# A two-block convolution on one core: float32 products in the first 1x1, shorter norm chains, a first 3x3 in pieces

## The reference

```
out = relu(bn(conv1x1(x, w1), g1, be1))        # 512 -> 128 channels
out = relu(bn(conv3x3(out, w2), g2, be2))      # 128 -> 128
out = bn(conv1x1(out, w3), g3, be3)            # 128 -> 512
x   = relu(x + softplus(residual_scale) * out)

out = conv1x1(x, v1) + bias1b
out = conv3x3(out + bias2a, v2) + bias2b
out = conv1x1(out + bias3a, v3) + bias3b
return relu(out * rscale + rbias + x)
```

## Time and profile before

| | us |
|---|---|
| median of 3 runs | 291.74 (290.62 to 291.79) |
| the profiled execution | 290.35, its span 288.3 |
| TensorE busy | 271.6 |
| VectorE busy | 250.2 |
| ScalarE busy | 203.0 |
| GpSimd busy | 15.9 |

### The profile page before, as it was taken

The page is one execution under the profiler, slowest core; times in us unless marked ns, Lnnn a source line. Parts: engine busy times, 40 slices in busy tenths (PEclk is TensorE's granted clock), DMA queues, the critical chain, the costliest instruction groups (busy, mean ns, idle before and its releaser), DMA issues.

```text
span 288.3 us, 4023 instructions
## 1 busy us (share of the span) xinstructions
PE 271.6 (94%) x1534; PEld 253.8 (88%) x1534; DVE 250.2 (87%) x384; ACT 203.0 (70%) x264; POOL 15.9 (6%) x23
## 2 busy tenths in 40 slices
PE   6878999899999998999997999999999999999991
PEld 3668998699999976868796999999999999999991
DVE  3599999999999657789699999999999997979593
ACT  5678883589877549819878783895976949573674
POOL 0000001000000009900000000000000000000000
PEclk9999999999999999999999999999999999999999
DMA  7999901300000010000000000004040050504088
GB/s 229 378 426 422 423 27 50 144 0 2 0 0 2 0 38 2 0 0 3 0 0 0 2 0 2 1 40 183 2 195 28 2 223 0 225 29 195 14 341 316
DMA packets 6818, 28.44 MB, mean 99 GB/s; under 512 B 912, under 2 KB 3472, under 8 KB 5904
## 3 DMA queue, kind: packets, MB, share of 16 engines
q1 hardware_dynamic: 6224, 27.78, 24.2%
q10 hardware_dynamic: 576, 0.41, 0.5%
HBM read 15.35 MB, written 12.85 MB: 98 GB/s over the span
## 4 chain that ended last, share of the span: by engine, by line
PE 79%; DVE 9%; ACT 6%; DMA 3%; issue 1%; SPq 1%; ACTq 0%; DVEq 0%
PE ps L1066 33%; PE ps L1052 18%; PE ps L1018 9%; PE ps L1055 9%; PE ps L1133 4%; DMA x<-x_dram 3%; PE ps L1116 2%; ACT x L556 2%; PE ps L1110 1%; DVE xl L650 1%; DVE xl L875 1%; ACT xh L357 1%; DVE x L870 1%; DVE vf L721 1%; PE ps L1027 1%
## 5 line engine op out<-in xcount | busy, mean ns | idle before, releaser
L511 ACT ACTIVATE x<-x,shift 128x784 f32<-128x784 f32 x32 | 29.9, 946 | 15.4 <-DVE x L870 15.2
L870 DVE SCALAR_TENSOR_TENSOR x<-ps,scale,x 128x784 f32<-128x784 f32 x32 | 32.4, 1030 | 1.3 <-PE ps L1055 1.2
L1066 PE MATMUL ps<-vh,wu0h 128*128 128x364 f32 (+1 forms) x96 | 32.0, 334 | 1.2 <-ACT vh L403 1.2
L1066 PE MATMUL ps<-vh,wu0l 128*128 128x364 f32 (+1 forms) x96 | 32.0, 333 | 0.0
L1066 PE MATMUL ps<-vh,wu1l 128*128 128x364 f32 (+1 forms) x96 | 32.0, 333 | 0.0
L1066 PE MATMUL ps<-vh,wu1h 128*128 128x364 f32 (+1 forms) x96 | 31.9, 333 | 0.0
L912 DVE SCALAR_TENSOR_TENSOR x<-ps,scal,x 128x784 f32<-128x784 f32 x31 | 31.5, 1028 | 0.0
L1066 PE MATMUL ps<-vl,wu0h 128*128 128x364 f32 (+1 forms) x96 | 31.3, 334 | 0.0
L875 DVE TENSOR_TENSOR xl<-x,xh 128x784 fp32r<-128x784 f32 x28 | 26.1, 971 | 5.8 <-ACT xh L518 5.8
L650 DVE TENSOR_TENSOR xl<-x,xh 128x1568 fp32r<-128x1568 f32 x13 | 23.2, 1781 | 1.8 <-ACT xh L357 1.8
L518 ACT ACTIVATE xh<-x 128x1568 fp32r<-128x1568 f32 x14 | 21.1, 1507 | 2.4 <-PE ps L1055 2.4
(11 more groups left out here) (206 smaller groups left out, 714.8 us busy)
## 6 DMA issues: line engine op xcount, KB each, us to landing
x<-x_dram SPq DMA_DIRECT2D x15, 784.0 KB, 8.2
out_dram<-x SPq DMA_DIRECT2D x6, 1568.0 KB, 5.2
out_dram<-x SPq DMA_DIRECT2D x7, 392.0 KB, 2.8
raw<-w_dram SPq DMA_DIRECT2D x1, 1088.0 KB, 5.1
raw<-w_dram SPq DMA_DIRECT2D x1, 576.0 KB, 11.3
raw<-w_dram SPq DMA_DIRECT2D x2, 256.0 KB, 3.1
x<-x_dram ACTq DMA_DIRECT2D x2, 196.0 KB, 4.0
x<-x_dram SPq DMA_DIRECT2D x2, 196.0 KB, 4.2
```

The costliest lines, as they stand in the source:

```text
L511: nc.scalar.activation(x_quad(q, c), x_quad(q, c), ACT.Relu, bias=shift3[:, c:c + 1]).then_inc(x1_ready, 1)
L870: nc.vector.scalar_tensor_tensor(x_quad(q, c), ps[:, bank:bank + 2, 0:N], scale3[:, c:c + 1], x_quad(q, c), ALU.mult, ALU.add).then_inc(s_ ...
L1066: return nc.tensor.matmul(by_row(ps[:, bank, 0:N])[:, :, a:RW - b], wu[part][:, TILE[k] + dw, :], by_row(v[:, k, :])[:, :, b:RW - a], star ...
```

## The change

- First 1x1. Units 0 and 1 are taken as float32 products of all four tiles, with no split; each unit from 2 to 15 takes its tile 0 as a float32 product and splits only tiles 1 to 3. Units 2, 3, 4 and 15 (`TILED`) are split tile by tile, the others three tiles at a time. The float32 tile waits only for the unit's landing, the split tiles for their low halves.
- The taps' transfer moves from behind unit 3 to behind unit 9; their sums move from unit 3 to units 10, 11 and 12, their high halves from unit 4 to units 11 and 13. par and scal move from the start of ScalarE's queue to the end of SyncE's loads.
- `keep_warm`: 10 at the start, none in units 0 and 1, 25 behind unit 15, 24 behind the first 3x3.
- First and second norm: `scale_shift1`, with the reciprocal of var_eps beside the root, then three dependent steps; shift in one step from a negated mean.
- Quad 0 of the first 3x3: activation by halves, sums, high and low halves by single tiles of 392 columns, the products tile by tile; the low half of the summed weights behind the sums.
- Later stage: conv_a(2, 0) goes ahead of conv_b(0, ...), and sum1(2, 0) ahead of low_x(1, 0).

The core of the diff:

```
@@ SyncE
             for u in range(1, XQ):
                 load_x(u)
-            sync.dma_start(raw[:, CT:CT + TAPS], w0_in[:, CT:CT + TAPS]).then_inc(w0u_loaded, 16)
...
                 load_x(u)
+                if u == 9:
+                    sync.dma_start(raw[:, CT:CT + TAPS], w0_in[:, CT:CT + TAPS]).then_inc(w0u_loaded, 16)
+            sync.dma_start(par[:, :], par_in).then_inc(par_loaded, 16)
+            sync.dma_start(scal[:, :], scal_in.rearrange("(a n) -> a n", a=1).to_broadcast([P, NSC])).then_inc(par_loaded, 16)
@@ ScalarE
-            act.dma_start(par[:, :], par_in).then_inc(par_loaded, 16)
-            act.dma_start(scal[:, :], ...).then_inc(par_loaded, 16)
...
+                act.wait_ge(*landed(u))
+                if u >= XS + 2:
                     act.wait_ge(conv1_done, u - XS + 1)
+                if u in TILED:
+                    for c in range(1, CT):
+                        nc.scalar.activation(xs0[u % XS][0][:, c, :], x[:, u, c, :], ACT.Copy).then_inc(xth_ready, 1)
+                else:
+                    nc.scalar.activation(xs0[u % XS][0][:, 1:CT, :], x[:, u, 1:CT, :], ACT.Copy).then_inc(xh0_ready, 1)
...
+            for k, rows in enumerate(even_odd(a1p[0])):
+                nc.scalar.activation(rows, y_unit(k), ACT.Relu, bias=shift1[:, 0:1], scale=scale1[:, 0:1]).then_inc(rows_ready, 1)
+            def first_high(k):
+                act.wait_ge(first_ready, k + 1)
+                nc.scalar.activation(v0h[0][:, k, :], v0f[0][:, k, :], ACT.Copy).then_inc(firsth_ready, 1)
+            first_high(0)
+            first_high(1)
             normalise1(1)
-            v0_high(0, 0)
-            v0_high(0, 1)
+            first_high(2)
+            first_high(3)
@@ VectorE
+            def scale_shift1(n, half_gamma, beta, scale, shift):
+                nc.vector.tensor_scalar(minus_mean[:, :], mean_off[:, 0:1], -1.0, None, ALU.mult)
+                dve.wait_ge(var_ready, n)
+                chain(nc.vector.reciprocal(r0[:, 0:1], var_eps[:, 0:1]))
+                dve.wait_ge(std_ready, n)
+                nc.vector.scalar_tensor_tensor(gr[:, 0:1], r0[:, 0:1], std[:, 0:1], half_gamma, ALU.mult, ALU.mult)
+                chain(nc.vector.scalar_tensor_tensor(vrr[:, 0:1], r0[:, 0:1], std[:, 0:1], std[:, 0:1], ALU.mult, ALU.mult))
+                chain(nc.vector.scalar_tensor_tensor(scale, vrr[:, 0:1], -3.0, gr[:, 0:1], ALU.add, ALU.mult))
+                nc.vector.scalar_tensor_tensor(shift, scale, minus_mean[:, 0:1], beta, ALU.mult, ALU.add).then_inc(bn_ready, 1)
...
-                nc.vector.scalar_tensor_tensor(mean_off[:, 0:1], mv[:, 0:1], bias, bias, ALU.add, ALU.subtract).then_inc(mean_ready, 1)
-                scale_shift(n, 1, half_gamma, beta, scale, shift)
+                chain(nc.vector.scalar_tensor_tensor(mean_off[:, 0:1], mv[:, 0:1], bias, bias, ALU.add, ALU.subtract))
+                scale_shift1(n, half_gamma, beta, scale, shift)
...
-            v0_sums(0)
-            v0_low(0, 0)
-            v0_low(0, 1)
+            for k in range(2):
+                dve.wait_ge(rows_ready, k + 1)
+                rows = padded(a1p[0])[:, k, :]
+                nc.vector.tensor_tensor(v0f[0][:, k, :], rows[:, 0:N], rows[:, RW:RW + N], ALU.subtract).then_inc(first_ready, 1)
+            even, odd = even_odd(a1p[0])
+            first_low(0)
+            nc.vector.tensor_tensor(v0f[0][:, 2, :], even, odd, ALU.add).then_inc(first_ready, 1)
+            first_low(1)
+            nc.vector.tensor_tensor(v0f[0][:, 3, :], odd, even, ALU.subtract).then_inc(first_ready, 1)
+            nc.vector.tensor_tensor(flat(wu0[1][:, 6:12, :]), ..., ALU.subtract).then_inc(u0l_ready, 1)
+            first_low(2)
+            first_low(3)
...
+            sum1(2, 0)
             low_x(1, 0)
             low_x(1, 1)
-            sum1(2, 0)
             sum1(2, 1)
@@ TensorE
+            def unit1(u):
+                bank = u % XS
+                if u >= XS:
+                    pe.wait_ge(y1_ready, u - XS + 1)
+                if u > 0:
+                    pe.wait_ge(*landed(u))
+                for c in range(CT if u < 2 else 1):
+                    if u == 0:
+                        pe.wait_ge(x0_loaded[c], 16)
+                    last = nc.tensor.matmul(ps[:, bank, 0:N], raw[:, c, :], x[:, u, c, :], start=c == 0, stop=u < 2 and c == CT - 1)
+                if u >= 2:
+                    for c in range(1, CT):
+                        if u in TILED:
+                            pe.wait_ge(xtl_ready, 3 * TILED.index(u) + c)
+                        elif c == 1:
+                            pe.wait_ge(xl0_ready, whole_units(u))
+                        h, l = xs0[u % XS][0][:, c, :], xs0[u % XS][1][:, c, :]
+                        for i, (a, v) in enumerate(((wa0[0], h), (wa0[1], h), (wa0[0], l))):
+                            last = nc.tensor.matmul(ps[:, bank, 0:N], a[:, c, :], v, start=False, stop=c == CT - 1 and i == 2)
                 last.then_inc(conv1_done, 1)
...
-            for q in range(3):
-                for c in range(CT):
-                    if q > 0:
-                        conv_a(q, c)
-                if q > 0:
-                    for c in range(CT):
-                        conv_b(q - 1, c)
+            for c in range(CT):
+                conv_a(1, c)
+            conv_a(2, 0)
+            for c in range(CT):
+                conv_b(0, c)
+            for c in range(1, CT):
+                conv_a(2, c)
+            for c in range(CT):
+                conv_b(1, c)
```

More of the change, by code:

```diff
@@ L140, in build @@
         g3s, be3s = small("g3s", CT), small("be3s", CT)
-        one = small("one", 1)
+        one, minus_mean = small("one", 1), small("minus_mean", 1)
         var_eps, std, r0, vrr, gr, mean_off = (small(n, CT) for n in ("var_eps", "std", "r0", "vrr", "gr", "mean_off"))
@@ L1019, in three @@
                 return last
-            def by_tile(bank, split, ready, dummies=(0, 0, 0, 0)):
-                for c in range(CT):
-                    keep_warm(dummies[c], BANKS - 1)
-                    pe.wait_ge(ready, c + 1)
-                    h, l = split[0][:, c, :], split[1][:, c, :]
-                    for i, (a, v) in enumerate(((wa0[0], h), (wa0[1], h), (wa0[0], l))):
-                        last = nc.tensor.matmul(ps[:, bank, 0:N], a[:, c, :], v, start=c + i == 0, stop=c == CT - 1 and i == 2)
-                return last
@@ L1047, in tile @@
+                last.then_inc(conv1_done, 1)
+            pe.wait_ge(warm_ready, 1)
+            keep_warm(10, BANKS - 1)
+            pe.wait_ge(w0_loaded, 16)
+            unit1(0)
+            unit1(1)
+            pe.wait_ge(w1l_ready, 1)
+            for u in range(2, U):
+                unit1(u)
+            keep_warm(25, BANKS - 1)
             def tile(bank, w, t, h, l, start, stop, low_ready):
@@ L1077, in product @@
                 return last
-            pe.wait_ge(u0l_ready, 1)
-            pe.wait_ge(v0h_ready, 1)
-            for k in range(2):
+            for k in range(4):
+                if k == 0:
+                    pe.wait_ge(u0l_ready, 1)
+                if k == 2:
+                    pe.wait_ge(u0l_ready, 2)
+                pe.wait_ge(firsth_ready, k + 1)
                 for dw in WINDOW:
@@ L1084, in _ @@
                         window(k, wu0, k, dw, part, v0h[0], dw == 1 and part == 0, False)
-            pe.wait_ge(v0l_ready, 1)
-            for k in range(2):
+                pe.wait_ge(firstl_ready, k + 1)
                 for dw in WINDOW:
@@ L1089, in _ @@
                 last.then_inc(conv2_done, 1)
-            pe.wait_ge(u0l_ready, 2)
-            for q in range(Q):
-                for k in range(0 if q > 0 else 2, 4):
-                    pe.wait_ge(v0l_ready, 2 * q + k // 2 + 1)
+            for q in range(1, Q):
+                for k in range(4):
+                    pe.wait_ge(v0l_ready, 2 * (q - 1) + k // 2 + 1)
                     if k == 0 and q > 1:
```

109 lines of the change are left out of this document (49 added, 60 removed).

## The result

The changed kernel takes 287.61 us (median of four runs, 287.01 to 288.15) against 291.70 (290.62 to 291.79). The ratio is 0.988, with an interval of 0.985 to 0.990, so it is 4.1 us faster; 6.6 were forecast, and 287.61 lies a hundredth beyond the end of the range (287.6). The profiled execution of the changed kernel is its slowest, 288.15 (span 286.0).

A forecast was written before the change was run, and what follows sets the result against it. Bound by loading and splitting before 24 us, TensorE to 48.2, small steps, then TensorE with VectorE close behind. First 1x1 4.9, first norm 0.56, first 3x3 0.6, second norm 0.5: 6.6 us, forecast 285.0, range 282.9 to 287.6.

The forecast's parts named there:

- Rival (2): First 1x1: changing between float32 and fp32r costs 0.26 us a unit more, 3.6 us in all; 288.7 us, chance 0.08.
- Rival (1): Start of the load: unit 1's load is not freed and lands at 9.65, 1.25 us less gain; 286.3 us, chance 0.18.
- Units 0 and 1 at the upper clock, from 5.3 us on: First 1x1: four float32 products take 2.64 us; unit 0 done at 7.95, unit 1 at 11.05.
- Rival (4): First 1x1: only unit 0 runs at TensorE's lower clock level; 287.2 us, chance 0.08.
- Unit 10 lands at 26.8, wanted at 29.4: Load in the first 1x1: with w0's taps behind unit 9, unit 10 still lands before TensorE needs it.
- First norm 0.56: Behind the first 1x1: the shorter chain of dependent steps takes 0.8 us instead of 1.36, gain 0.56.
- Second norm 0.5: Same steps as the first norm; an extra wait for mean_off costs about 0.05 us, gain 0.5.
- First 3x3 product at t0 + 1.7: t0 is the end of the first norm's shift; pieces of 392 start the 3x3 at t0 + 1.7 instead of t0 + 3.11.
- Net gain 0.6: First 3x3: start 1.4 us earlier less 0.7 waited for VectorE, taken as 0.6; bounds 0 and 1.4.
- Dummies cost nothing: Filler matmuls, at the start and behind first 1x1 and 3x3: fewer cost nothing while the clock stays at its upper level.
- Rival (3): First 1x1: TensorE stays at its lower clock level for the first three units, losing the gain; 292.3 us, chance 0.03.
- matmuls 0.33 apart past 6 us: First 1x1: one of two signs named as showing the forecast wrong; the other was TensorE idle in units 5 to 15.

The follow-up runs named there:

- e14: Kernel before with only the first 1x1's part of the change (float32 products, moved transfers and weight sums); old chains, pieces, tile and later dummies: 287.02 us, ratio 0.986.
- e9: Kernel after with the 25 and 24 dummies behind the first 1x1 and first 3x3 as 50 and 48 of half the length: 286.71 us, ratio 0.985.
- e4: Kernel after with 13 dummies instead of 10 ahead of unit 0, and par and scal back at the start of ScalarE's queue: 288.26 us, ratio 0.989.
- e10: Kernel after without its ten dummies ahead of unit 0: 288.05 us, ratio 0.988.
- e1: Kernel after, unchanged, run once more as the base: 287.25 us, ratio 0.986 to the kernel before.
- e2: Kernel after with 13 dummies instead of 10 ahead of unit 0: 287.16 us, ratio 0.986.
- e6: Kernel after with the low halves of the transformed weights made in the first 1x1, out of quad 0's pieces: 286.28 us, ratio 0.985.
- e7: Kernel after with the old chains of both norms and the moved tile put back: 286.96 us, ratio 0.987.
- e15: Kernel after with nine dummies in TensorE's 1.98 us wait near 149 us, a repeat for its profile: 285.94 us, ratio 0.983.
- e5: Kernel before, unchanged, profiled a second time: 290.58 us, ratio 1.000.
- e8: Kernel after with the taps' transfer behind unit 12, its sums two units later, and four one-column fills on VectorE ahead of the second norm: 286.72 us, ratio 0.986.
- e3: Kernel after with par and scal back at the start of ScalarE's queue: 287.40 us, ratio 0.988.

## Why the prediction was wrong, step by step

Of the 6.6 us, 4.1 came. The missing 2.5, with the runs that sized each part: 0.8 in the first 1x1 (e14), 0.6 to 0.7 in the output (e9), 0.17 in the first norm, 0.6 in the second, 0.33 in the first 3x3 (the last three from the first profile). No single step carries the miss; the one below that had the mechanism wrong, and not a size alone, is the clock under unit 0.

- *Float32 product 0.66, unit 2.29, no price of the change of format:* right (0.66, 2.27). Rival (2) fell.
- *Unit 1 lands at 8.4, since q10's small packets slow the load:* right, and shown by e4 (9.6 with them back). Rival (1) fell.
- *Units 0 and 1 at the upper clock, from 5.3 us on:* the step that failed. It was concluded from dummies 0.17 apart at 5.80, in one execution; in half of the 14 profiles with the change's first 1x1 the record of the granted clock begins at 6.4 to 10.5 us, in six of them past 9.0, and unit 0 runs wholly or in part at the lower level. With a late rise the last product comes at 44.5 to 44.9 (after, e9, e10, e14), with an early one at 43.3 to 44.2 (e1, e2, e6, e7, e15), where 43.3 was forecast. So the late rise costs about 0.9 where it strikes and half of that on the average; about as much of the 0.8 belongs to the load, below. The kernel before hides this behind its load (e5); the changed one shows it, because it made TensorE the bound there. Rival (4), given 0.08 and 287.2, has this mechanism and the nearest number. That its number is near is in part luck: it priced a low unit 0 at 2.2 us, of which 0.7 reach the last statistics (after against e1), and the rest of the distance came from the other steps. It was drawn as a fault that happens or not. It is a spread that each execution draws from. (The first eleven dummies were read as 0.31 apart; the weight loads have them 0.33 apart, which is the same level.)
- *Unit 10 lands at 26.8, wanted at 29.4:* mis-sized by 1.1 to 1.7 (27.9 and 28.5). A fetch of q8 lies at 26 us in these two traces and holds one of the engines that unit 10 needs, and in e8 unit 11 is late in the same way; that the fetch is the cause was not tried alone. It takes back 0.4 to 0.9 of an early clock.
- *First norm 0.56:* 0.39, of which the new chain gives 0.26 (e7) and 0.13 has no known source. The working took each new step at the old length; an operation with two tensors as scalars takes 0.22 (gr, vrr, shift above) against 0.16.
- *Second norm 0.5:* -0.1. The hole of 0.4 ahead of gr is new. e8 shows that it can go; then the norm gains 0.2.
- *First 3x3 product at t0 + 1.7:* 2.12. ScalarE's two row pieces take 1.32, and VectorE starts on the first at t0 + 0.85, not at 0.57. *VectorE at quad 1 at t0 + 5.6:* 5.81. *Net gain 0.6:* 0.27. The working had the low half in VectorE's list and asked what it costs, not whether it fits the wait ahead of it. e6 gives 0.9.
- *Dummies cost nothing:* wrong by a way that wasn't on the list, and the output, where the 0.6 to 0.7 were lost, had no term in the sum at all. Dummies are instructions, and their number decides where in the kernel the fetches lie.
- *The moved tile is worth nothing:* right, and for the reason given (e7).
- Rival (3) fell: no profile shows three units at the lower clock. In e3, the latest, it lasted for about one.

What would have shown it: the prediction named "matmuls 0.33 apart past 6 us" as its mark of failure. That mark is ill drawn, since the two records of a float32 product are 0.33 apart at the upper level too; weight loads 0.65 apart, as they are up to 8.82, are the one that tells.

## What to carry to other kernels

When a change takes away the wait that bounded a stretch, ask what that wait was hiding: here it hid the moment at which the clock rises, and one profile can't show a spread. Count instructions as well as time; a dummy removed in one stage can move a 16 KB fetch into the full output of another. A small piece of a busy engine belongs ahead of that engine's last wait, not behind it.

## What was not expected of the hardware

- The record of the granted clock begins at 3.9 to 10.5 us in executions of nearly the same start, with ten or thirteen dummies ahead (4.9 and 6.4 with thirteen), and at 9.1 in the one profile with none.
- One fetch of 16 KB of instructions holds a DMA engine for 1.06 us; amid the output's transfers their median time to landing is 0.9 us longer (3.7 instead of 2.8).
- TensorE's 1.98 us of idle time is followed, in some executions, by 3.41 us at a granted clock of 0.50, cost 1.3 us. With 1.67 us of it filled, none of 23 has the mean clock that goes with it.
- The same instruction with the same operands starts 0.14 or 0.51 us behind the one before it, by its place in the stream. The cause stays open, as does what decides the moment of the rise.
